# A transformer block in one kernel: who splits q and k into high and low parts

## The reference

```python
x = x + layernorm(attention(layernorm(x)))
x = x + layernorm(moe(layernorm(x)))

# attention, causal, T = 1024, dh = 64
q, k, v = x @ Wq, x @ Wk, x @ Wv                # 16 heads of 64
logits = (q @ k.T + causal + pos_bias) / dh
out = softmax(logits) @ v                        # heads side by side
return out @ Wo + bo
# moe: shared gelu MLP + 8 gelu MLPs, each row weighted by a top-2 gate
```

## Time and profile before

| what | before |
|---|---|
| median of three runs | 875.44 us |
| the profiled execution: time of the fastest run, and its span | 874.59 us, 874.6 us |
| TensorE matmul busy | 775.7 us (89%) |
| VectorE busy | 716.2 us (82%) |
| ScalarE busy | 624.6 us (71%) |
| GpSimd busy | 265.7 us (30%) |
| chain that ended last: TensorE, VectorE, ScalarE, DMA | 70%, 12%, 6%, 4% |

### The profile page before, as it was taken

How to read it: one execution, slowest core, us unless ns; L and a number is a source line. 1 busy time by engine, 2 the same in 40 slices (tenths; PEclk the granted TensorE clock), 3 DMA queues, 4 the chain that set the end, 5 groups by cost and what they waited for, 6 DMA issues and landing times.

```text
span 874.6 us, 17078 instructions
## 1 busy us (share of the span) xinstructions
PE 775.7 (89%) x4453; PEld 661.3 (76%) x4453; DVE 716.2 (82%) x1610; ACT 624.6 (71%) x1366; POOL 265.7 (30%) x285
## 2 busy tenths in 40 slices
PE   2988299999999999999999999998379999999993
PEld 2667288888888888888888888887367877777772
DVE  6648088888888888888888888888869899999886
ACT  2557177877887787787778778778386776667764
POOL 2220223323332332332332233222401344444421
PEclk9999699999999999999999999999779999999997
DMA  8769534324423423432442342341001221122101
GB/s 218 261 227 111 76 72 93 78 60 89 91 60 84 95 61 69 93 78 60 88 92 60 84 95 61 69 92 50 31 1 48 76 73 72 72 72 72 49 1 48
DMA packets 61993, 71.74 MB, mean 82 GB/s; under 512 B 40020, under 2 KB 50960, under 8 KB 58896
## 3 DMA queue, kind: packets, MB, share of 16 engines
q1 hardware_dynamic: 56944, 67.73, 30.9%
q0 software_dynamic: 720, 2.12, 2.9%
q10 hardware_dynamic: 4304, 1.58, 0.8%
HBM read 28.35 MB, written 9.53 MB: 43 GB/s over the span
## 4 chain that ended last, share of the span: by engine, by line
PE 70%; DVE 12%; ACT 6%; issue 5%; DMA 4%; ACTq 1%; DVEq 0%; POOL 0%; SPq 0%; POOLq 0%
PE out_ps L1214 16%; PE trans_ps L1196 15%; PE score_ps L1181 12%; PE shared_ps L1226 6%; DMA q_hl<-k_hl 3%; DVE pT_lo L973 3%; PE score_ps L1086 3%; PE score_ps L1088 3%; PE score_ps L1087 3%; DVE pT_lo L873 3%; ACT pT_hi L670 2%; PE trans_ps L1086 2%; PE trans_ps L1088 2%; PE trans_ps L1087 2%; PE shared_ps L1086 2%
## 5 line engine op out<-in xcount | busy, mean ns | idle before, releaser
L670 ACT ACTIVATE pT_hi<-trans_ps 128x512 fp32r<-128x512 f32 (+3 forms) x384 | 185.8, 493 | 77.8 <-PE trans_ps L1196 38.0
L655 ACT ACTIVATE probs<-score_ps,row_min 128x128 f32<-128x128 f32 (+7 forms) x256 | 190.4, 744 | 53.1 <-DVE row_min L860 52.8
L873 DVE TENSOR_TENSOR pT_lo<-trans_ps,pT_hi 128x512 fp32r<-128x512 f32 (+3 forms) x384 | 202.0, 554 | 31.1 <-ACT pT_hi L670 29.6
L860 DVE CUSTOM_DVE_ANT_0 score_ps<-score_ps,bias 128x128 f32<-128x128 f32 (+7 forms) x256 | 194.4, 759 | 39.3 <-PE score_ps L1181 36.6
L1196 PE MATMUL trans_ps<-ident,probs 128*128 128x128 f32 x1152 | 191.1, 275 | 20.1 <-DVE pT_lo L873 19.8
L1181 PE MATMUL score_ps<-k_hl,q_hl 128*128 128x512 f32 (+2 forms) x768 | 183.6, 353 | 19.7 <-DMA k_hl<-k_hl 19.1
L467 POOL TENSOR_TENSOR acc<-acc,head_out 128x512 f32<-128x512 f32 x64 | 82.4, 1288 | 316.8 <-DVE head_out L891 288.3
L1196 PEld LDWEIGHTS trans_ps<-ident,probs 128*128 128x128 f32 x1152 | 138.0, 141 | 44.4 <-DVE pT_lo L873 28.0
L1181 PEld LDWEIGHTS score_ps<-k_hl,q_hl 128*128 128x128 f32 x768 | 135.1, 189 | 40.8 <-issue 19.5
L1214 PE MATMUL out_ps<-pT_hi,v_hl 128*128 128x512 f32 (+2 forms) x384 | 156.8, 409 | 1.1 <-DVE pT_lo L873 1.1
L973 DVE TENSOR_TENSOR pT_lo<-probs,pT_hi 128x512 fp32r<-128x512 f32 x144 | 133.1, 953 | 23.8 <-ACT pT_hi L732 15.6
(11 more groups left out here) (135 smaller groups left out, 1156.2 us busy)
## 6 DMA issues: line engine op xcount, KB each, us to landing
q_hl<-k_hl SPq DMA_DIRECT2D x64, 256.0 KB, 3.6
k_hl<-k_hl SPq DMA_DIRECT2D x32, 512.0 KB, 4.2
v_scratch<-probs SPq DMA_DIRECT2D x16, 512.0 KB, 3.1
v_raw<-v_scratch SPq DMA_DIRECT2D x32, 256.0 KB, 4.5
bias_all<-gate_scratch SPq DMA_DIRECT2D x8, 1024.0 KB, 4.9
bias_all<-bias_scratch SPq DMA_DIRECT2D x1, 2048.0 KB, 9.1
v_raw<-in_L_ffn_Wfc SPq DMA_DIRECT2D x8, 256.0 KB, 4.8
bias<-in_L_ffn_Wproj SPq DMA_DIRECT2D x8, 256.0 KB, 5.1
```

The costliest lines, as they stand in the source:

```text
L655: act.activation(probs[s % 4][:, 0:n], scores_of(s % QB)[:, 0:n], ACT.Exp, bias=row_min[:, s:s + 1], scale=-1.0, accum_out=row_sum[:, s:s ...
L670: act.activation(pT_hi[c][:, CH * g:CH * g + m, q * P:(q + 1) * P], trans_ps[k % 2][:, 0:m * P].rearrange("p (m q) -> p m q", q=P), ACT.Co ...
L860: dve.tensor_tensor_reduce(out=ps, in0=ps, in1=bias_b[b][:, T - n:T], scale=1.0, scalar=3e38, op0=ALU.add, op1=ALU.min, accum_out=row_min[ ...
L873: dve.tensor_tensor(pT_lo[c][dst], trans_ps[k % 2][:, 0:m * P].rearrange("p (m q) -> p m q", q=P), pT_hi[c][dst], ALU.subtract).then_inc(p ...
```

## The change

ScalarE now copies each half of q and k out of the accumulator as plain 32 bit values into a new tile `qk_raw` (one for each half), and that copy alone frees the bank. GpSimd then makes the high part (a cast) and the low part (a subtraction) from `qk_raw`. The wait for the scores that still read the old k moves from ScalarE to GpSimd. VectorE's subtraction is gone. `place_q` waits for `qk_lo` as before, which GpSimd now counts.

```diff
+        qk_raw = [sb(f"qk_raw{i}", [P, W]) for i in range(NC)]
...
+            def split_qk(h, b, half):
+
+                n = h * (2 * B) + 2 * b + half
+                cols = slice(half * W, (half + 1) * W)
+                pool.wait_ge(qk_raw_ready, n + 1)
+                if not (isinstance(h, int) and h == 0):
+                    pool.wait_ge(scores_ready, h * S + QB * b + QB - S)
+                pool.sem_inc(pool_passed, 1)
+                pool.tensor_copy(k_hl[b][:, 0, cols], qk_raw[half][:]).then_inc(qk_hi, 1)
+                pool.wait_ge(qk_hi, n + 1)
+                pool.sem_inc(pool_passed, 1)
+                pool.tensor_tensor(k_hl[b][:, 1, cols], qk_raw[half][:], k_hl[b][:, 0, cols],
+                                   ALU.subtract).then_inc(qk_lo, 1)
...
+                if s in QK_SLOT:
+                    nxt, b, half = QK_SLOT[s]
+                    if not (nxt and last):
+                        split_qk(h + nxt, b, half)
...
+            split_qk(0, 0, 0)
+            split_qk(0, 0, 1)
             pool.wait_ge(bias_turned, N_TURN)
             take_bias(0, 0)
             split_v(0, 0)
...
-            def split_qk_hi(h, b, half):
+            def evacuate_qk(h, b, half):
                 act.wait_ge(qk_psum, h * (2 * B) + 2 * b + half + 1)
-                if not (isinstance(h, int) and h == 0):
-                    act.wait_ge(scores_ready, h * S + QB * b + QB - S)
-                act.activation(k_hl[b][:, 0, half * W:(half + 1) * W], shared_ps[:], ACT.Copy).then_inc(qk_hi, 1)
+                if not (isinstance(h, int) and h == 0 and b == 0):
+                    act.wait_ge(qk_lo, h * (2 * B) + 2 * b + half + 1 - NC)
+                act.activation(qk_raw[half][:], shared_ps[:], ACT.Copy).then_inc(qk_raw_ready, 1)
...
-            def split_qk_lo(h, b, half):
-                cols = slice(half * W, (half + 1) * W)
-                dve.wait_ge(qk_hi, h * (2 * B) + 2 * b + half + 1)
-                dve.tensor_tensor(k_hl[b][:, 1, cols], shared_ps[:], k_hl[b][:, 0, cols],
-                                  ALU.subtract).then_inc(qk_lo, 1)
...
                 if kind == "qk":
-                    pe.wait_ge(qk_lo, n * (2 * B) + 2 * b + part + 1)
+                    pe.wait_ge(qk_raw_ready, n * (2 * B) + 2 * b + part + 1)
```

More of the change, by code:

```diff
@@ L252, in transformer_block @@
         qk_psum = sem("qk_psum")
+        qk_raw_ready = sem("qk_raw_ready")
         qk_hi = sem("qk_hi")
@@ L631, in _ @@
             nT_evac(0, 3)
-            split_qk_hi(0, 0, 0)
+            evacuate_qk(0, 0, 0)
             copy_v(4)
             copy_v(5)
-            split_qk_hi(0, 0, 1)
+            evacuate_qk(0, 0, 1)
             act.activation(std[:], rstd[:], ACT.Exp)
@@ L693, in slot @@
                     if not (nxt and last):
-                        split_qk_hi(h + nxt, b, half)
+                        evacuate_qk(h + nxt, b, half)
             for s in range(S):
@@ L840, in _ @@
             nT_evac(0, NCH - 1)
-            split_qk_lo(0, 0, 0)
             copy_v(4)
             copy_v(5)
-            split_qk_lo(0, 0, 1)
             for t in range(6, NB):
@@ L906, in slot @@
                         do(h - 1, *slots[s + S])
[L907 to L910, removed]
             for s in range(S):
@@ L1134, in _ @@
             values_of_all(5)
-            pe.wait_ge(qk_lo, 1)
+            pe.wait_ge(qk_raw_ready, 1)
             project_qk(0, 0, 1)
@@ L1155, in wait_shared @@
                 if isinstance(h, int) and h == 0 and not uses:
-                    pe.wait_ge(qk_lo, NC)
+                    pe.wait_ge(qk_raw_ready, NC)
                     return
```

## The result

The changed kernel takes 876.79 us (median of 20 runs, 876.17 to 877.68) against 875.55 us before (20 runs, 873.62 to 876.6): a ratio of 1.0015, 95% interval 1.0008 to 1.0021. By the bound of the prediction (1.8 us) that is no change that can be told; the interval leaves out 1, so over 20 runs a loss of 1.2 us is clear of the noise. The time is 0.1 us from the forecast. Behind it stand a loss and a gain, as forecast, though neither had quite the size forecast.

A forecast was written before the change was run, and what follows sets the result against it. Bound by a chain mostly over TensorE, with a turn of TensorE, ScalarE and VectorE and an 18.52 us stall before head 1. 874.6 - 3.7 + 5.0 = 875.9, plus 0.8 to the median: 876.7 us; range 873.8 to 885.5.

The forecast's parts named there:

- ScalarE's copy costs nothing: ScalarE's copy out of the accumulator: same count and shape, only the written type differs, so no time change.
- The bank, 3.7 us gained: Second half's projection: bank free 0.7 us earlier, about 0.13 us back in each of 29 halves, 3.7 us (3.2 to 4.4).
- VectorE's relief is nothing: Loop, 120 to 600 us: VectorE loses 56 subtractions of 0.69 us, which gains nothing.
- GpSimd's pair, 1.3 us later, 0.5 of slack left: Loop: GpSimd's cast and subtraction deliver qk_lo 1.3 us later; of 1.8 us slack 0.5 stays, so barely hidden.
- Rival B: Loop slack used up: TensorE waits 0.3 us at the start of each of 29 units, 885.4 us; chance 0.08.
- Head 0, 5.0 us lost: Head 0: GpSimd's splits delay copies and loads; slot 8 starts near 77, head 1 at 109.2, 5.0 us lost.
- the prediction's own bounds: Loss in head 0: +3.9 for the shift of the loads alone, +5.7 for that of k's copy alone.
- the count of DMA work: Head 0: loads 28.5, k's copy 2.9, v's load 1.1 us, added from 69.5, end at 102.0, 5.0 later.
- the bound of 79: Head 0, ahead of slot 8: k's copy was to land between 74.2 and 79 us.
- Turns packet by packet?: DMA queues, head 0: the skill's rule that engines alternate between queues by packet, trusted only if a whole transfer counts as one.
- Rival A: Head 0: k's copy falls behind bo, slot 8 at 100.8, head 1 at 119.4, 885.1 us; chance 0.20.
- Rival C: Head 0 costs nearly nothing: bo ends 1.0 us later, 872.7 us; chance 0.12, including VectorE's relief being worth more.

## Why the prediction was right, step by step

- *ScalarE's copy costs nothing.* Right: 0.61 us as before.
- *The bank, 3.7 us gained.* Right in mechanism, but too large: 3.1 measured from head 1 on, and only 2.8 of it in the units. The gate gave 0.11 and 0.16 us, as forecast (0.13), but only 0.097 of it reaches the end of a unit.
- *VectorE's relief is nothing.* Right for the wait that it spoke of (17.6, then 17.4 us). As a general claim it is too strong: with an instruction of 0.69 us at that place VectorE gates the transposes, and where b = 0 the bank's gain is gone. The prediction looked for who waits for L820 and not for what would wait next, once L820's own gate was away.
- *GpSimd's pair, 1.3 us later, 0.5 of slack left.* Right in outcome (hidden), and a narrower thing than stated: 1.55 us later, 0.09 to 0.26 left. The sum took 0.09 us from cast to subtraction, as in v's split; here it is 0.18, as it was in the split of the weights in the trace of before. It had nothing for GpSimd's start, 0.19 us behind ScalarE. Rival B did not happen, but its point was nearer than thought: TensorE begins to wait after some 0.2 us more and not after 0.5. Its price was right in kind: 0.56 us of delay cost 0.35 a unit (12.3 us on the span, 1.7 of it in head 1's first unit).
- *Head 0, 5.0 us lost.* Right in place and in kind: two stalls, the second where the first had been. Their sizes were the other way round: 13.5 us ahead of slot 8 where about 9 were forecast, 9.3 ahead of head 1 where about 13 were. The size of the loss was 3.8, just below the prediction's own bounds (3.9 to 5.7). The step that failed is the count of DMA work: it added k's 2.9 and v's 1.1 us to the 28.5 of the loads, as if the engines took one after the other. In the traces the packets of Wo and bo run from 68.7 to 96.4 us before and from 70.1 to 100.1 now: a start 1.4 us later (1.0 forecast), but only 2.3 us more in length and not 4.0. K's copy landed at 79.46, after the expected 77 and just past the bound of 79. The queues of the changed kernel from 73 to 79 us (packets, MB, share of 16 engines):

```profile
q1 hardware_dynamic: 636, 0.67, 57.4%
q0 software_dynamic: 189, 0.68, 53.2%
```

  The shares add up to 110.6%, with a packet counted whole where it starts; with the packets cut at the ends of the stretch it is still 107.2%. So packets overlap in time on an engine, and their times must not be added. That is not a matter of two queues alone: q0 by itself, counted the second way, had 103.5% from 70.9 to 73.9 us in the kernel before. How the 1.7 us were saved in detail is not shown. From 79 to 98 us nearly all of the share is one queue's:

```profile
q0 software_dynamic: 193, 0.79, 99.5%
q1 hardware_dynamic: 146, 0.04, 0.9%
```

  k's copy, issued 0.3 us ahead of bo, got its 0.52 MB through beside Wo and the start of bo (the 0.67 MB above have a part of v's load in them). The rest of v's load, in packets of 256 bytes, went slowly beside bo, and q's copy, behind it in the same queue, took 13.36 us.
- *The two errors cancel*: the loss was put 1.2 us too high and the gain 0.6 too high, so the profiled sum was 0.6 too high (875.9 against 875.3). The step from there to the median was 0.7 too low: the prediction added 0.8 us, and the median of the changed kernel lies 1.5 above its profiled span. It had taken the span of 874.6 us for the run of 874.59. But in every run of which both are on record the time is 1.7 to 2.1 us above the span, so that span belongs to an execution of about 876.4 us (an estimate, 874.6 + 1.8), and it is not true that next to nothing lies around it. The 0.1 us between forecast and median is luck.
- *Turns packet by packet?* The prediction named the rule of the Trainium skill's page "DMA: Bandwidth & Descriptors" and trusted it only if a whole transfer counts as the packet. Where packets of both queues moved, they agree with the rule better than that: 193 packets of q0 to 146 of q1 from 79 to 98 us, and 85 to 77 from 84 to 93.2 us with bo issued ahead of k's copy. By time it is no even share (99.5% to 0.9%), since a packet of bo held an engine for some 1.6 us (99.5% of 16 x 19 us, by 193) and a small one of v's for hardly any. What the rule does not explain is the time ahead of a transfer's first packet: q's copy, issued at 75.67 in the kernel before, moved nothing until 95 us, and k's with bo ahead of it nothing for 10 us. That stays open.
- *Rival A* did not happen but is real: two microseconds of GpSimd's order separate the change from it, and it costs 9 us. Its forecast of slot 8 (100.8) and head 1 (119.4) is met by 99.35 and 118.22, though not by its mechanism as stated: most of k's copy moved while bo was under way. *Rival C* (872.7) would have needed k's copy to fit beside the loads for nothing. What would have made it nearly true is another order in GpSimd's stream, at 104.92.

## What to carry to other kernels

When work moves to an engine with slack, ask three times: what it delays in that engine's own stream (here the three loads, which nobody thinks of as work), what the thing it fed has left (here 1.8 us, of which 1.55 went), and what waits next where a gate is opened. A stall elsewhere can hide a cost completely: the same change costs 0.7 us with bo's stall behind it and 11 us without. And look at the stall itself first: not loading one row 16 times over was worth 21 us, seven times what the change gains in the whole loop.

## What was not expected of the hardware

- The repeated load is slow for its size: after 79 us it moved 0.79 MB in 19 us, some 42 GB/s, at a share of 99.5% of the DMA engines. In the kernel before, its packets of 4096 bytes took 1.47 us on the mean (76 to 95 us), where packets of the same size, nearly all of them Wo's, took 0.31 (68.5 to 74 us). Both loads are made of rows of 512 bytes; bo's is the same row each time. That this repetition is the cause was not tested. GpSimd spreads the same row over the same tile in 1.91 us.
- Where GpSimd waits for its own last instruction, the next one starts 0.18 us after its end in the split of q and k (56 times, 10.1 us in all) but 0.08 in the split of v (59.40 + 0.61, then 60.09). In the program the first has one instruction more between the wait and the subtraction, a count (`pool_passed`); whether that is the cause was not tested.
- VectorE and GpSimd slowed each other where both worked from on-chip memory to on-chip memory. In the kernel where VectorE splits the first halves, its subtraction took 0.69 us with GpSimd idle and 0.98 beside v's split, and GpSimd's 1.59 instead of 1.27:

```profile
55.89 0.69 DVE L846 TENSOR_TENSOR k_hl<-qk_raw,k_hl 128x512 fp32r<-128x512 f32 x1
...
58.95 0.98 DVE L846 TENSOR_TENSOR k_hl<-qk_raw,k_hl 128x512 fp32r<-128x512 f32 x1
```

```profile
59.47 1.59 POOL L471 TENSOR_TENSOR v_hl<-v_raw,v_hl 128x512 fp32r<-128x512 f32 x1
...
62.90 1.27 POOL L471 TENSOR_TENSOR v_hl<-v_raw,v_hl 128x512 fp32r<-128x512 f32 x1
```

- After a long stall the granted clock of TensorE does not come back after a fixed time: near 108 us after a start at 104.15, and at 110 after one at 104.39. So the length of head 1's first unit (18.23, 18.28 and 19.20 us in three of the kernels) is no measure of a change.
